# Dropping the reciprocal copies and reordering the second tile's first MLP chunk in a decoder layer

## The reference

```python
# 1: gated linear recurrence over the tokens
a = sigmoid(x @ Wf.T);  b = silu(x @ Wi.T) * (1 - a)
h = linear_scan(a, b)
xg = h * silu(x @ Wg.T)
x = layernorm(x + (xg * rsqrt(mean(xg**2) + eps) * w_norm) @ Wo.T)
# 2: a weighted running mean of the context v, keys k = x
y_t = (p_t + exp(u + k_t) * v_t) / (q_t + exp(u + k_t))   # p, q decay by w per step
x = layernorm(x + y)
# 3: MLP with 8-bit rounded inputs, weights and hidden rows
gate_up = q(x) @ q(w_gate_up).T
x = layernorm(x + q(silu(gate) * up) @ q(w_down).T)       # 1408 hidden columns
```

## Time and profile before

| what | value |
|---|---|
| median of 3 runs | 411.18 us (409.6 to 411.26) |
| profiled execution | 412.55 us, of it the span of instructions 410.1 us |
| TensorE busy | 370.8 us (90%) |
| VectorE busy | 353.6 us (86%) |
| ScalarE busy | 318.7 us (78%) |
| GpSimd busy | 219.3 us (53%) |
| granted TensorE clock, mean | 0.981 |

### The profile page before, as it was taken

One profiled execution on the slowest core, in us unless ns is written; L12 is line 12 of the kernel. 1 busy time (PEld: TensorE's weight loads), 2 busy tenths in 40 slices (PEclk: granted clock), 3 DMA queues, 4 the chain that ended last, 5 costly groups with the idle time before them and its releaser, 6 DMA issues.

```text
span 410.1 us, 7960 instructions
## 1 busy us (share of the span) xinstructions
PE 370.8 (90%) x2774; PEld 289.9 (71%) x2774; DVE 353.6 (86%) x639; ACT 318.7 (78%) x420; POOL 219.3 (53%) x281
## 2 busy tenths in 40 slices
PE   7699899889997899999999999999999999659992
PEld 7698799768964788669775977497749785335541
DVE  3879898888788988988899988998899889898895
ACT  3677599769848989599959996799769994974782
POOL 1546772753355725674377535673566356644561
PEclk9989999999999999999999999999999999959999
DMA  7977456011110013000500050004000300000002
GB/s 257 361 273 269 164 195 243 2 53 27 59 46 0 2 48 134 0 28 2 179 2 27 2 179 2 26 0 154 25 0 26 129 0 0 26 2 18 36 26 77
DMA packets 12842, 31.74 MB, mean 77 GB/s; under 512 B 2038, under 2 KB 5132, under 8 KB 12812
## 3 DMA queue, kind: packets, MB, share of 16 engines
q1 hardware_dynamic: 12812, 31.35, 21.9%
HBM read 27.14 MB, written 4.21 MB: 76 GB/s over the span
## 4 chain that ended last, share of the span: by engine, by line
ACT 25%; PE 24%; issue 15%; DVE 14%; POOL 10%; POOLq 0%; ACTq 0%; DVEq 0%
PE proj_ps L530 13%; PE slot_ps L639 8%; POOL ring L1352 4%; ACT L1056 3%; ACT hqT L1021 2%; ACT ring L1014 2%; ACT L1060 2%; DVE inp L1545 2%; DVE x_max L1670 2%; ACT gate L897 2%; POOL gate L1292 2%; ACT q_state L962 2%; ACT q_state L956 2%; ACT gate L935 1%; ACT xqT L998 1%
## 5 line engine op out<-in xcount | busy, mean ns | idle before, releaser
L639 PE MATMUL slot_ps<-w1q,xqT 128*128 128x512 bf16 (+1 forms) x384 | 83.1, 367 | 5.1 <-DVE ring L1702 2.9
L1352 POOL TENSOR_TENSOR ring<-ring 128x512 f32<-128x512 f32 (+1 forms) x48 | 59.6, 1248 | 42.3 <-ACT ring L1007 41.1
L639 PEld LDWEIGHTS slot_ps<-w1q,xqT 128*128 128x128 bf16 x384 | 36.0, 99 | 44.7 <-issue 4.4
L530 PE MATMUL proj_ps<-x_high,proj_high 128*128 128x256 f32 x384 | 65.3, 292 | 1.7 <-DVE inp L1567 1.0
L530 PE MATMUL proj_ps<-x_high,proj_low 128*128 128x256 f32 x384 | 62.2, 284 | 0.0
L530 PE MATMUL proj_ps<-x_low,proj_high 128*128 128x256 f32 x384 | 62.0, 283 | 0.0
L530 PEld LDWEIGHTS proj_ps<-x_high,proj_high 128*128 128x128 f32 x384 | 53.6, 190 | 3.8 <-issue 1.6
L530 PEld LDWEIGHTS proj_ps<-x_high,proj_low 128*128 128x128 f32 x384 | 53.5, 191 | 0.0
L530 PEld LDWEIGHTS proj_ps<-x_low,proj_high 128*128 128x128 f32 x384 | 53.0, 189 | 0.0
L1327 POOL TENSOR_TENSOR den<-den,q_state 128x512 f32<-128x512 f32 x16 | 21.2, 1328 | 49.3 <-ACT q_state L962 48.9
L1007 ACT ACTIVATE ring<-ring,zero_bias,x_scale 128x512 f32<-128x512 f32 (+1 forms) x48 | 37.0, 775 | 9.5 <-DVE ring L1699 9.4
(11 more groups left out here) (157 smaller groups left out, 835.5 us busy)
## 6 DMA issues: line engine op xcount, KB each, us to landing
ring<-w_gate_up_dram SPq DMA_DIRECT2D x11, 512.0 KB, 4.2
forget<-xT_dram SPq DMA_DIRECT2D x8, 512.0 KB, 3.4
x_sb<-x_dram SPq DMA_DIRECT2D x8, 512.0 KB, 3.8
c_sb<-cT_dram SPq DMA_DIRECT2D x8, 512.0 KB, 4.5
out_dram<-late SPq DMA_DIRECT2D x12, 256.0 KB, 2.1
late<-w_down_dram SPq DMA_DIRECT2D x2, 704.0 KB, 6.9
ring<-w_down_dram SPq DMA_DIRECT2D x2, 704.0 KB, 4.2
scale_rows<-scratch_dram SPq DMA_DIRECT2D x2, 704.0 KB, 6.0
```

The source lines that it names most:

```text
L530: last = nc.tensor.matmul(out, a, b, start=(i == 0), stop=(i == len(terms) - 1))
L639: last = nc.tensor.matmul(slot_ps[:, s, half * 512:half * 512 + width], xqT[:, par, d, t * P:(t + 1) * P], w1q[:, d, half * I + at:half * ...
L1352: nc.gpsimd.tensor_tensor(hid, hid, gate_buf[:, at:at + width], ALU.mult).then_inc(hid_ready, 1)
```

## The change

Four edits. The copy of the reciprocal into PSUM (place_reciprocal) goes, in all rounds, at the start and at the end; the division reads the reciprocal where ScalarE wrote it, in SBUF, and waits for rec_copy_ready. On TensorE the projections 4 and 5 go ahead of chunk 0 of the second tile. On VectorE the scaling of that chunk goes from before the divisions to behind gating. On ScalarE normalise_3 of tile n - 2 goes from behind read_hidden to ahead of read_projection(b + 2, 2).

```diff
@@ TensorE, iteration
                 mlp_down(n - 1, 1)
-                mlp_up(b, par, 1, [0])
                 project(b + 2, 4)
                 project(b + 2, 5)
+                mlp_up(b, par, 1, [0])
                 mlp_up(b, par, 1, [1])
                 mlp_up(b, par, 1, [2])
@@ ScalarE
-            def place_reciprocal(b, h):
-
-                act.wait_ge(rec_copy_ready, 2 * b + h + 1)
-                act.wait_ge(num_ready, 2 * b + h + 1)
-                nc.scalar.activation(blocks(turn_feat, h), blocks(rec_copy, h), ACT.Identity,
-                                     bias=zero_bias[:, :]).then_inc(rec_ready, 1)
@@ ScalarE, iteration
                 silu(b, par, 0, [2])
+                normalise_3(n - 2, 0)
                 read_projection(b + 2, 2)
                 forget_gate(b + 2)
                 read_hidden(n - 1, 1, 0)
                 read_hidden(n - 1, 1, 1)
-                normalise_3(n - 2, 0)
                 read_projection(b + 2, 3)
                 exp_tables()
                 logarithm(b + 1, 0)
                 logarithm(b + 1, 1)
                 reciprocal(b + 1, 0)
-                place_reciprocal(b + 1, 0)
                 reciprocal(b + 1, 1)
-                place_reciprocal(b + 1, 1)
@@ ScalarE, start (batches 0 and 1) and end (batch 7)
-            place_reciprocal(0, 0)
-            place_reciprocal(0, 1)
...
-            place_reciprocal(1, 0)
-            place_reciprocal(1, 1)
...
-            place_reciprocal(7, 0)
-            place_reciprocal(7, 1)
@@ VectorE
             def divide(b, h):
 
-                dve.wait_ge(rec_ready, 2 * b + h + 1)
+                dve.wait_ge(rec_copy_ready, 2 * b + h + 1)
                 dve.wait_ge(num_ready, 2 * b + h + 1)
                 nc.vector.tensor_tensor(blocks(turn_feat, h)[:, :, 1:], blocks(num, h)[:, :, 1:],
-                                        blocks(turn_feat, h)[:, :, 1:],
+                                        blocks(rec_copy, h)[:, :, 1:],
                                         ALU.mult).then_inc(y0_ready, 1)
@@ VectorE, iteration
                 read_down(n - 1, b - 1, 1)
-                scale_products(b, 1, [0])
                 divide(b + 1, 0)
                 divide(b + 1, 1)
                 refine(b + 1, 0)
                 refine(b + 1, 1)
                 layer_norm_3(n - 1, 1)
                 gating(b + 2)
+                scale_products(b, 1, [0])
                 scale_products(b, 1, [1])
```

More of the change, by code:

```diff
@@ L335, in decoder_layer @@
         rec_copy_ready = sem("rec_copy_ready")
-        rec_ready = sem("rec_ready")
         newton_ready = sem("newton_ready")
```

## The result

The changed kernel takes 414.59 us (median of 6 runs, 413.56 to 417.42); the kernel before, run beside it, 410.93 (6 runs, 409.46 to 413.56). The ratio is **1.0099**, 95% interval 1.0052 to 1.0146: 1.0% slower. The profiled execution of the changed kernel has a span of 411.7 us against 410.1.

What follows compares the result with a forecast made beforehand. TensorE was taken to bound the round almost alone. Rounds plus start gave 4.0 + 0.75 = 4.8 or 2.75 + 1.8 = 4.6 us; +4.5 was taken on the median 411.18, giving 415.7 us, range 408.2 to 417.6.

Steps and rivals of the forecast that it cites:

- Parts 1 and 2: ScalarE: removing the copies saves 1.5 us and the earlier normalisation 0.26 us on the path to the gate reads.
- Part 3: TensorE: projections ahead of the MLP chunk end at 201.6, so gating can start at 202.5 at the earliest; 0.35 us gain.
- Part 4: VectorE: scaling behind gating, with the silu, makes the state rounding start 2.6 us behind gating's start instead of 1.26.
- rival C: Gate reads stay tied to something else, gating stays at 204.19, rounding 1.34 later; five rounds +6.7, 417.9 us; chance 0.03.
- Part 5: Divisions with two SBUF inputs and newton on GpSimd hold each other; a round costs 0.55 to 0.8 us more.
- one and one: Divisions and newton alternate: gating at 203.4, state rounding 0.55 late; start 1.8, +4.6 us in all.
- the row at 74.46: Profile row where a GpSimd instruction stood by through both VectorE instructions; basis for both divisions first, +4.8 us.
- g: Gating's start in the round: break-even 202.85, earliest 202.5, forecast 203.4 (one and one) or 203.65 (both first).
- chunk 2's stall: TensorE: chunk 2 waits for the scaling, which frees its PSUM slot, and is 1.1 to 1.3 us late.
- both first: Both divisions run before newton's second: gating at 203.65, state rounding 0.8 late; start 0.75, +4.8 us in all.
- A: No contention between divisions and newton: gating at 202.5, rounding 0.3 sooner, -2.9 us in all, 408.3 us; chance 0.20.
- B: Contention but small: gating at 202.9 to 203.1, rounding 0.05 to 0.25 late, 411.8 to 412.7 us; chance 0.16.

Runs made afterwards that it cites:

- number 10: Number 1 with normalise_3 back at its old place behind read_hidden, both moves kept; 410.71 us, ratio 1.0007 to the kernel before.
- number 1: The changed kernel with the division's numerator left in PSUM, reciprocal still read from SBUF; 407.8 us, ratio 0.994 to the kernel before.
- Number 3: The kernel before with only the projections and the scaling moved, copies kept; 417.81 us, ratio 1.0174.
- number 7: The changed kernel with newton on GpSimd made to wait for both divisions, operands unchanged; 424.63 us, ratio 1.0342 to the kernel before.
- 8: Number 1 repeated unchanged, on one chip with 9 and 10; 409.14 us, ratio 0.996 to the kernel before.
- 5: Number 1 with the silu of the second tile's chunk 0 put behind the state rounding on ScalarE; 415.59 us, ratio 1.0105 to the kernel before.
- 6: Number 1 with projections and scaling back at their old places; 410.01 us, ratio 0.9978 to the kernel before.
- 9: Number 6 repeated, on one chip with 8 and 10; 410.05 us, ratio 0.999 to the kernel before.
- number 4: The changed kernel with the silu of the second tile's chunk 0 behind the state rounding on ScalarE; 421.04 us, ratio 1.0292 to the kernel before.

## Why the prediction was right, point by point

**The time.** 415.7 was forecast and 414.59 measured; against the runs before, +1.1% forecast and +0.99% measured. The profiled spans differ by 1.6 us only; the changed kernel's was 1.3 us ahead at the first gating (33.62 against 34.94), before any changed step has run, and counted from there the difference is 2.9. From state rounding to state rounding it divides so: 0.31 in the first stretch, 0.90 in the second, 0.27 up to the first round, 1.66 in the next four, and 0.21 less in the end. The prediction's terms add up to 4.5. So the mechanism was right, but its terms were too large by about a half of what the profiles show, and that the time came within 1.1 us of the forecast is partly luck: the interval of the ratio, 0.5 to 1.5%, takes in both 2.9 and 4.5 us.

**Parts 1 and 2** came out as worked out: the read at 193.71 is 0.31 us sooner at the same place of TensorE (forecast 0.26), the gate reads 1.83 us (201.06 against 202.89), forecast 1.76. That the normalisation's move is needed was shown only with the contention gone (number 10).

**Part 3**, the earliest gating at the end of the gate read, is what number 1 shows: 0.4 us off a round, against 0.35 forecast.

**Part 4**, the 2.6 us from gating to the state rounding: 206.01 - 203.43 = 2.58. Number 3 shows it alone: 1.43 a round (1.34 forecast for rival C).

**Part 5** was the step that decided, and it held: the pair of divisions held from both sides, newton and the residual as well. Of the two orders the prediction left open, the runs show one and one; the row at 74.46, on which the other order rested, did not carry over. The Trainium skill (SBUF — State Buffer, "Who interferes with whom") says that whoever issues first has the shared ports for the whole instruction and the other is blocked. The trace agrees as far as that goes: the second division and newton's second each end only after the instruction that was there first. Who comes next when both engines have more to do the page does not say, so that the order one and one was the prediction's own step.

g was forecast at 203.4 for this order and is 203.43 on the clock of this trace, but 203.17 at TensorE's own pace, 0.23 sooner. Most of it is a misread row: newton's first was taken to last 1.37 us, from its start at 197.79 to the second's at 199.16. In the kernel before, the second had to wait for the second exponential (ScalarE's timeline), which is over at 199.09; the first itself took 1.27.

```profile
198.38 0.71 ACT L962 ACTIVATE q_state<-q_state,zero_bias 128x512 f32<-128x512 f32 x1
```

In the changed kernel both exponentials are early and the second newton starts 1.22 us behind the first.

**The size of a round** was taken too large: 0.55 to 0.8 us forecast, 0.42 measured (43.12 against 42.70), so 1.9 us over five rounds (0.27 and 1.66) instead of 2.7 to 4.0. The sized terms are the state rounding, 0.30 late instead of 0.55, and chunk 2's stall, 0.77 instead of 1.1 to 1.3. Of the signs, these came: the first gate read 4.4 us behind the first exponential, and no idle time for ScalarE ahead of gating. The others came smaller or not quite: the first division 0.89 (over 0.9 forecast; the second took 1.78), newton's second 1.73 (2.3 belongs to the other order), the wait before chunk 2 0.6 to 0.8 instead of 1.2, 0.3 us left before the input transposes, and a round of 43.12 instead of 43.3 to 43.5.

**The start** was forecast at 0.75 (both first) or 1.8 (one and one). The stretch with batch 1's divisions shows 0.9, where one and one was forecast at 1.2. The held divisions go with it: the stretch takes 42.57, 42.61 and 42.61 in the three kernels that have them, 41.65 and 41.67 with the copies; in number 7 the divisions are free and the wait for newton takes their place (42.71). In the six kernels with the numerator in PSUM gating starts after 41.22 to 41.26 but is then held itself, and by the state rounding they take 42.25 to 42.28. So the free divisions give back only 0.3 us here. The stretch with batch 0's divisions (first gating to second) was 0.3 longer, where 0.6 was forecast for one and one. It can't be pinned on them: the same start code gave 36.9 in numbers 1, 8 and 10 and 35.4 in numbers 5, 6 and 9, the same again in each repetition, and I can't say why.

**Rivals.** A, no contention, is refuted by 1 and 7. Its time would have been 408.3, a ratio of 0.993; number 1, the change without contention at the divisions, took 407.8 and in its repetition 409.14 (0.994 and 0.996), so A's arithmetic was about right and its premise wrong. B's time was ruled out by the interval, but its mechanism only just: gating at 203.17 and the rounding 0.30 late lie nearer to B's bounds (203.1 and 0.25) than to the forecast's 203.4 and 0.55. C's condition, gating tied to the old gate read, did not come about in the changed kernel; number 3 has it, and took 417.81 where C gives 417.9.

## What to carry to other kernels

Before a VectorE operand is moved from PSUM to SBUF, or an instruction with two SBUF inputs is moved in time, look at what GpSimd does in the same microseconds: here removing two copies of 0.69 us made two divisions 1.3 us longer and newton and the residual behind them 0.3 to 0.4 us. The remedy was to leave the other operand in PSUM, where it already was. A step that frees an engine is worth nothing until the chain behind it can start sooner, and a reordering that relies on that should be tried together with it: the moves alone cost 1.4 us a round; with free divisions they gain 0.2, by the profiles.

## What the runs showed of the hardware

I had expected the one-and-one order as a possibility only. The pair took 2.58 or 2.59 us in all five rounds, and instructions of about 0.6 and 1.2 us in alternation made a VectorE division of 690 ns last up to 1781. The held time is counted as busy: VectorE's busy time rose from 353.6 to 364.3 us with 639 instructions in both, and no wait or idle row names it. Only the duration against the same instruction elsewhere shows it. And a GpSimd instruction can do more harm later than earlier: with a silu that came 0.5 us later behind gating (number 4) the two subtractions took 3.19 us against 1.43 in the changed kernel.
